# Second self attention: ScalarE seeds the score banks, and the values follow each slot

## The reference

```python
q = (h @ wq).reshape(b, n, 16, 64).transpose(0, 2, 1, 3)   # k and v alike, from the same h
scores = jnp.einsum('bhnd,bhld->bhnl', q, k) * 64 ** -0.5
probs = jax.nn.softmax(scores, axis=-1)
out = jnp.einsum('bhnl,bhld->bhnd', probs, v)
return out.transpose(0, 2, 1, 3).reshape(b, n, 1024) @ wo + bo
```

## Time and profile before

| What | Value |
|---|---|
| median of 3 runs | 4223.74 us |
| lowest and highest | 4218.38 and 4226.12 us |
| span of the profiled execution, first to last instruction | 4217.9 us |
| second self attention, first transfer to last projection (about) | 1905 to 3436 us |
| mean granted TensorE clock over the span | 0.952 |
| PE, DVE, ACT, POOL busy over the span | 93%, 66%, 44%, 44% |

### The profile page before, as it was taken

How to read it: one execution, slowest core, us unless ns; L and a number is a source line. 1 busy time by engine, 2 the same in 40 slices (tenths; PEclk the granted TensorE clock), 3 DMA queues, 4 the chain that set the end, 5 groups by cost and what they waited for, 6 DMA issues and landing times. The chain is left out here.

```text
span 4217.9 us, 64445 instructions
## 1 busy us (share of the span) xinstructions
PE 3909.5 (93%) x24639; PEld 2598.3 (62%) x24639; DVE 2770.9 (66%) x4547; ACT 1839.2 (44%) x2746; POOL 1859.2 (44%) x1203
## 2 busy tenths in 40 slices
PE   3799999994998997998999999999999979999899
PEld 2533443433557886884666666666666647777787
DVE  6599999953536654435676767676766737665665
ACT  1267777771443333442333333333333334444333
POOL 1288970001203002005777777877787753222200
PEclk9789999996779998997999999999999989999899
DMA  4734434405622005883211111121112010000100
GB/s 159 180 56 77 59 57 48 42 2 94 102 43 52 22 13 197 306 308 103 75 51 51 64 63 51 51 76 51 51 51 76 26 31 10 10 10 1 42 15 17
DMA packets 314421, 294.96 MB, mean 70 GB/s; under 512 B 133420, under 2 KB 237292, under 8 KB 313860
## 3 DMA queue, kind: packets, MB, share of 16 engines
q1 hardware_dynamic: 311460, 281.88, 25.7%
q0 software_dynamic: 2656, 8.97, 0.7%
HBM read 161.92 MB, written 127.28 MB: 69 GB/s over the span
## 5 line engine op out<-in xcount | busy, mean ns | idle before, releaser
L1741 POOL TENSOR_TENSOR f_sums<-f_sums,f_probs 128x1024 f32<-128x1024 f32 x384 | 915.5, 2384 | 154.8 <-ACT f_probs L1860 117.1
L1860 ACT ACTIVATE f_probs<-f_st 128x1024 f32<-128x1024 f32 x512 | 525.0, 1027 | 938.7 <-PE f_st L1906 933.9
L1758 DVE TENSOR_REDUCE f_mx<-f_s 128x1 f32<-128x512 f32 x1024 | 659.8, 686 | 380.7 <-PE f_s L1883 369.4
L1369 DVE TENSOR_REDUCE f_mx<-f_s 128x1 f32<-128x512 f32 x1024 | 638.6, 683 | 50.8 <-PE f_s L1501 28.4
L1481 ACT ACTIVATE f_probs<-f_st 128x512 f32<-128x512 f32 x1024 | 535.9, 601 | 225.6 <-PE f_st L1518 225.5
L1883 PE MATMUL f_s<-f_k,f_q 64*128 64x512 f32 x3072 | 515.0, 415 | 18.6 <-DMA f_k<-k 12.5
L1906 PE MATMUL f_st<-f_q,f_k 64*128 64x512 f32 x3072 | 485.2, 390 | 1.1 <-ACT f_probs L1860 1.0
L1920 PE MATMUL f_acc<-f_probs,f_v 128*64 128x512 f32 x2048 | 465.0, 596 | 0.0
L1883 PEld LDWEIGHTS f_s<-f_k,f_q 64*128 64x128 f32 x3072 | 341.2, 189 | 166.6 <-issue 112.1
L1906 PEld LDWEIGHTS f_st<-f_q,f_k 64*128 64x128 f32 x3072 | 366.4, 184 | 25.9 <-ACT f_probs L1860 3.8
L1518 PE MATMUL f_st<-f_q,f_k 50*128 50x512 f32 x1024 | 332.7, 472 | 6.9 <-ACT f_probs L1481 6.8
(11 more groups left out here) (320 smaller groups left out, 7874.5 us busy)
## 6 DMA issues: line engine op xcount, KB each, us to landing
q<-f_stage SPq DMA_DIRECT2D x80, 512.0 KB, 2.9
k<-f_stage SPq DMA_DIRECT2D x80, 512.0 KB, 2.9
f_q<-q SPq DMA_DIRECT2D x32, 1024.0 KB, 5.0
f_k<-k SPq DMA_DIRECT2D x32, 1024.0 KB, 7.3
v<-f_v_stage SPq DMA_DIRECT2D x64, 256.0 KB, 3.1
f_v<-v SPq DMA_DIRECT2D x32, 512.0 KB, 8.5
f_q<-q SPq DMA_DIRECT2D x96, 128.0 KB, 4.2
f_k<-k SPq DMA_DIRECT2D x96, 128.0 KB, 6.9
```

The source lines that it names most:

```text
L1369: v.tensor_reduce(mx[:, i % 2, c:c + 1], bank[u % 4][:, :], AX_X, ALU.max).then_inc(s_free, 1)
L1741: g_.tensor_tensor(out, out, probs[:, n % NP, :, :], ALU.add).then_inc(sum_done, 1)
L1758: v.tensor_reduce(mx[:, i % 2, c:c + 1], bank[u % 3][:, :], AX_X, ALU.max).then_inc(s_free, 1)
L1860: a_.activation(probs[:, s % NP, :, :], stb[s % 2][:, :, :], ACT.Exp, scale=L.scale).then_inc(p_ready, 1)
```

## The change

- `shifted` has 3 x 2 matmuls; the fourth product is gone, with `mones` and `m`. In its place ScalarE copies the negative maxima, held on all 128 partitions in `shift`, into the double bank (128 x 1024) after the exp that emptied it (`seed`), and the matmuls add to what stands there. `prime` issues four matmuls once at the start.
- `turned` is one copy on VectorE in place of two operations. `maxima` writes 8 KB to DRAM, waits, and then reads it back onto 128 partitions, 1 MB, by one transfer a step, in place of four small ones.
- GROUP goes from 4 to 1. TensorE's list for each slot is one shifted set, one pair, and the values of the slot two back. `weigh` stands in slots 1 and 9 behind the pair, the projections in slots 7 and 15 behind the pair, `turn` at the start of slot 8. The first values of a half stand in slots 2 and 10.
- EARLY goes from 3 to 8: pairs run up to 24 ahead, and 8 of step 1 are issued before the first slot.
- On VectorE the reciprocal stands behind the pair of its slot. q and k are loaded once the shifted sets of step i - 1 are issued, v once its values are done.

```diff
-        NP, DEPTH, GROUP, EARLY, RING0 = 8, 3, 4, 3, 3
+        NP, DEPTH, GROUP, EARLY, RING0 = 8, 3, 1, 8, 3
+        BLOCKS, PER_HALF, LAG = SLOTS // GROUP, KC // GROUP, 2
...
+        def next_pair(i, s):
+            n, j = (i + 1, EARLY + s) if s < SLOTS - EARLY else (i + 2, s - SLOTS + EARLY)
+            return (n, j) if n < STEPS else None
...
+        def turn_at(i, b):
+            return i + 1 if b == (SLOTS - EARLY) // GROUP and i + 1 < STEPS else None
...
+        def den_at(i, b):
+            if b == PER_HALF + 1:
+                return i, 0
+            return (i - 1, 1) if b == 1 and i > 0 else None
...
+        def y_at(i, b):
+            if b == BLOCKS - 1:
+                return i, 0
+            return (i - 1, 1) if b == PER_HALF - 1 and i > 0 else None
...
+        def values_at(i, b):
+            if b >= LAG:
+                return i, b - LAG
+            return (i - 1, BLOCKS + b - LAG) if i > 0 else None
...
-            m = [sb(f"m{k}", [P, N], F32R) for k in two]
-            mones = sb("mones", [P, P], F32R)
+            shift = [sb(f"shift{k}", [P, 2, N]) for k in two]
...
                 def maxima(i):
                     par = i % 2
-                    sp.wait_ge(m_split, i + 1)
-                    for h in range(2):
-                        for r in range(2):
-                            row = 64 * h + r
-                            sp.dma_start(m[par][row:row + 1, :].bitcast(F32).rearrange("o (q t) -> o q t", t=P),
-                                         mm[par][h * QB:(h + 1) * QB, r, :]).then_inc(m_in[par], 16)
+                    sp.wait_ge(s_free, at["turn", i] + 1)
+                    if i >= 2:
+                        sp.wait_ge(m_in[par], 16 * (i // 2))
+                    sp.dma_start(self.shift[par].rearrange("(c t) -> c t", t=P), mm[par][:, :]).then_inc(m_out[par], 16)
+                    sp.wait_ge(m_out[par], 16 * (i // 2 + 1))
+                    if i >= 2:
+                        sp.wait_ge(seeded, (i - 1) * SLOTS)
+                    sp.dma_start(shift[par][:, :, :].rearrange("p h t -> p (h t)"), self.shift[par].partition_broadcast(P))\
+                        .then_inc(m_in[par], 16)
...
-                sp.wait_ge(set_done, 6)
...
-                            sp.wait_ge(pv_done, i * GROUP)
+                            sp.wait_ge(st_ready, i * SLOTS)
                         load(i + 2)
+                        if i > 0:
+                            sp.wait_ge(pv_done, i * BLOCKS)
+                        load_values(i + 2)
...
-                        dve.wait_ge(m_in[par], i // 2 * 64)
-                    v.tensor_scalar(mm[par][:, 0, :].bitcast(U32), rows.bitcast(U32), HI12, None,
-                                    ALU.bitwise_and).then_inc(m_cut, 1)
-                    dve.wait_ge(m_cut, i + 1)
-                    v.tensor_tensor(mm[par][:, 1, :], rows, mm[par][:, 0, :], ALU.subtract).then_inc(m_split, 1)
-                    dve.wait_ge(m_split, i + 1)
-                    dve.sem_inc(s_free, 1)
+                        dve.wait_ge(m_out[par], 16 * (i // 2))
+                    v.tensor_copy(mm[par][:, :], rows).then_inc(s_free, 1)
...
-                    dve.wait_ge(pv_done, 2 * n + 2)
+                    dve.wait_ge(pv_done, (n + 1) * PER_HALF)
...
+                    for b in range(BLOCKS):
+                        if turn_at(i, b):
                             negate(i + 1)
+                            turned(i + 1)
+                        for s in range(GROUP * b, GROUP * b + GROUP):
+                            if next_pair(i, s):
+                                pair(*next_pair(i, s))
+                        if y_at(i, b):
+                            k, half = y_at(i, b)
+                            project(2 * k + half)
+                        if den_at(i, b):
+                            k, half = den_at(i, b)
+                            invert(2 * k + half)
+                        if values_at(i, b) and values_at(i, b)[1] % PER_HALF == PER_HALF - 1:
+                            k, grp = values_at(i, b)
+                            normalise(2 * k + grp // PER_HALF)
...
-                act.sem_inc(p_ready, 2)
...
+                def seed(n):
+                    i, s = n // SLOTS, n % SLOTS
+                    half = s // KC
+                    if n >= 2:
+                        act.wait_ge(p_ready, n - 1)
+                    if s == 0:
+                        act.wait_ge(m_in[i % 2], 16 * (i // 2 + 1))
+                    a_.activation(stb[s % 2][:, :, :], shift[i % 2][:, :, half * HALF:(half + 1) * HALF], ACT.Copy).then_inc(seeded, 1)
...
+                act.wait_ge(primed, 1)
+                seed(0)
+                seed(1)
...
                         a_.activation(probs[:, s % NP, :, :], stb[s % 2][:, :, :], ACT.Exp, scale=L.scale).then_inc(p_ready, 1)
-                        if s == 5 and i > 0:
+                        if n + 2 < STEPS * SLOTS:
+                            seed(n + 2)
+                        if s == 4 and i > 0:
                             high(2 * i - 1)
-                        if s == 13:
+                        if s == 12:
                             high(2 * i)
...
+                def prime():
+                    pe.wait_ge(q_in[0], 32)
+                    for k in two:
+                        for h in range(2):
+                            ins = t.matmul(stb[k][:, h, :], k_[0][:, 0, 0:P], q[0][:, 0, 0:HALF], start=True, stop=True)
+                    ins.then_inc(primed, 1)
...
                 def shifted(i, s):
-                    cur, par, half, c = i % DEPTH, i % 2, s // KC, s % KC
-                    if s == 0:
-                        pe.wait_ge(m_in[par], (i // 2 + 1) * 64)
-                    pe.wait_ge(p_ready, i * SLOTS + s + 1)
+                    cur, half, c = i % DEPTH, s // KC, s % KC
+                    pe.wait_ge(seeded, i * SLOTS + s + 1)
                     cols, keys = slice(half * HALF, (half + 1) * HALF), slice(c * P, (c + 1) * P)
-                    for r, (kk, qq) in enumerate(((0, 0), (0, 1), (1, 0), (None, None))):
+                    for r, (kk, qq) in enumerate(((0, 0), (0, 1), (1, 0))):
                         for h in range(2):
                             rows = slice(64 * h, 64 * h + 64)
-                            lhs = mones[rows, :] if kk is None else k_[cur][rows, kk, keys]
-                            rhs = m[par][rows, cols] if kk is None else q[cur][rows, qq, cols]
-                            ins = t.matmul(stb[s % 2][:, h, :], lhs, rhs, start=r == 0, stop=r == 3, tile_position=(64 * h, 0))
+                            ins = t.matmul(stb[s % 2][:, h, :], k_[cur][rows, kk, keys], q[cur][rows, qq, cols], start=False, stop=r == 2,
+                                           tile_position=(64 * h, 0), skip_group_check=True)
                     ins.then_inc(st_ready, 1)
...
-                    pe.wait_ge(p_ready, i * SLOTS + GROUP * grp + GROUP + 2)
-                    if grp % 2 == 0 and 2 * i + grp // 2 > 0:
-                        pe.wait_ge(on_done, 2 * i + grp // 2)
+                    pe.wait_ge(p_ready, i * SLOTS + GROUP * grp + GROUP)
+                    half = 2 * i + grp // PER_HALF
+                    if grp % PER_HALF == 0 and half > 0:
+                        pe.wait_ge(on_done, half)
...
+                prime()
...
                 for i in range(STEPS):
-                    for s in range(SLOTS):
-                        shifted(i, s)
-                        if s == 3 and i > 0:
-                            weigh(i - 1, 1)
-                            values(i - 1, 3)
-                        if s == 7:
-                            if i > 0:
-                                project(2 * i - 2)
-                            values(i, 0)
-                        if s == 11:
-                            weigh(i, 0)
-                            values(i, 1)
-                        if s == 15:
-                            if i + 1 < STEPS:
-                                turn(i + 1)
-                            if i > 0:
-                                project(2 * i - 1)
-                            values(i, 2)
-                        if s < SLOTS - EARLY:
-                            if i + 1 < STEPS:
-                                pair(i + 1, EARLY + s)
-                        elif i + 2 < STEPS:
-                            pair(i + 2, s - SLOTS + EARLY)
+                    for b in range(BLOCKS):
+                        if turn_at(i, b):
+                            turn(i + 1)
+                        shifted(i, b)
+                        if next_pair(i, b):
+                            pair(*next_pair(i, b))
+                        if y_at(i, b):
+                            k, half = y_at(i, b)
+                            project(2 * k + half)
+                        if den_at(i, b):
+                            weigh(*den_at(i, b))
+                        if values_at(i, b):
```

(17 more changed lines are left out.)

67 lines of the change are left out of this document (25 added, 42 removed).

## The result

The changed kernel takes 4456.98 us, the median of 4 runs (4446.76 to 4463.29); the kernel before took 4224.57 beside it. The ratio is 1.0553, with an interval of 1.0532 to 1.0573. The profiled execution took 4461.46 us with a span of 4459.2, so 241.3 us are to be found against the span before.

A forecast was written before the change was run, and what follows sets the result against it. TensorE's list, busy 1409.97 of 1410 us at full clock, was taken to set the end. Terms of -118 + 173 + 119 + 14 + 7 - 4 = +191 took the span from 4217.9 to 4409; forecast 4415 us, range 4290 to 4480.

The forecast's parts named there:

- Step 1: Shifted sets on TensorE: 512 slots lose one product for both heads, 118 us less.
- Step 2: Values behind each slot: 384 more round trips between 64-row and 64-column tiles at 0.45 us, 173 us more.
- Step 3: Handover of `acc` between halves: TensorE waits 1.89 us for VectorE's multiply, 63 times, 119 us more.
- The rival of the clock: A tenth of TensorE's work runs at 1.2 GHz because of gaps: 154 us more, 4569 us; chance 0.04.
- Step 4: The turn in slot 8: one more tile change and a wait for `negate`, 31 x 0.45 = 14 us more.
- Step 5: Start and end: five early pairs cost 7 us more, a shorter final wait for POOL saves 4 us.
- What was taken as free: ScalarE's seeds, taken as 1.03 us each, the shift through DRAM and POOL's adds were to add no time.
- no drain at this grain: Rival: all 512 round trips between tile shapes cost nothing, 4213 us; chance 0.08 with its weaker forms.
- the handover is hidden: Rival: the chain behind `weigh` is covered and step 3 is nothing, 4296 us; chance 0.08.
- ScalarE's pace: Rival: seeds of 2.5 us make ScalarE pace the slots, 4588 us; chance 0.03.
- a late shift: Rival: the shift lands 6 us late in each step, 4600 us; chance 0.03.

The follow-up runs named there:

- e6: The changed kernel's order with the fourth product and its rows m back in place of ScalarE's seeds: 4496.78 us, ratio 1.0655.
- e12: e11 plus two one-column matmuls of zero weights on 64-column tiles between shifted set and pair, in 14 of 16 slots: 4562.09 us, ratio 1.0808.
- e2: The changed kernel with eight products of zero weights per head ahead of the pair before each handover: 4376.34 us, ratio 1.0367.
- e11: e2 with one product of zero weights per head ahead of each handover instead of eight: 4374.69 us, ratio 1.0377.
- e3: The changed kernel with the first values of each half one slot later, beside the second ones: 4387.82 us, ratio 1.0403.
- e1: The changed kernel, but ScalarE copies `acc` to SBUF; the multiply reads that copy and the next values wait only for the copy: 4468.91 us, ratio 1.059.
- e5: e1 with the multiply of a half placed on VectorE behind the reduces of the following slot's pair: 4261.35 us, ratio 1.0104.
- e9: The changed kernel in two-slot blocks (pair, set, set, pair, values), multiply between the next block's first reduces, projections one block later: 4183.23 us, ratio 0.9918.
- after: The changed kernel itself, with no further edit, against the kernel before: 4456.98 us, ratio 1.0553.
- e7: The changed kernel with GROUP 4, bursts of four slots and then their values, seeds and EARLY 8 kept: 4627.31 us, ratio 1.0958.

## Why the prediction came out as it did

The direction and most of the size were right: forecast 4415, measured 4457. The 241 us of the span against the 191 of the sum, step by step:

- **Step 1, the product.** 512 x 0.231 = 118 us, as forecast: sets have six records, and e6, which puts the product back, has slots 0.24 longer.
- **Step 2, the changes of shape.** Right in kind, too dear in size. Slots start 2.60 us apart (sets at 2501.33, 2503.94 and 2506.54), and the pieces are worth 6 x 0.231 + 0.86 = 2.25. A trip so costs 0.36: 0.15 from values to set (1.01 for 0.86), 0.11 in the set (0.80 for 0.69) and 0.10 in the pair ahead of the values. The 0.20 on the way in, read ahead of `weigh`, was the term that was too large. With 0.36 for the new trips and 0.45 for the old, the step is 512 x 0.36 - 128 x 0.45 = 127 us for the 173 forecast. e12 measures 0.42 with a visit that also has a few ns of columns.
- **Step 3, the handover.** 128.2 us in 63 waits for 119 forecast, 2.01 each for 1.89. VectorE's chain took 5.38 for 5.48, and 0.15 more to the start of the values, which the forecast left out; PE had nothing to do from 3.52 for 3.59.
- **What step 3 left out: the clock.** This is the term that failed. The forecast took the clock as 1.00 and left its fall to a rival with 0.04, "as the row of the start shows that it takes much more idling than forecast". That row had PE two thirds busy; nothing in it said that less idling would be free. Behind 47 of 53 waits of 2.01 us TensorE runs at half clock for 3.4 us, at 1.5 us a time, and e2 and e11 give back 91.5 and 89.4 us of the span (80.6 and 82.3 of the median) by filling the wait or 0.23 us of it. The Trainium skill ("TensorE: Matmul & The Clock Gate", Why this matters for your kernels) warns that idle gaps between bursts of matmuls bring the slow clock back. The trace agrees in kind, but here shorter gaps than the page's rule names are enough: one of 2.01 us at a time, in e3 two of 0.5 and 0.8. The rival of the clock had the mechanism right, and its 154 us came from a guess that a tenth of the work would be slow.
- **Step 4, the turn.** The transpose starts at 2510.91 and the next set at 2511.12, without a wait, as `negate` had ended (0.18 from 2510.67) by then. 31 x 0.21 = 7 us for 14.
- **Step 5, start and end.** The first shifted set starts at 1951.32, before at 1951.85, with five more pairs ahead of it; but the stage's loads were issued 5.1 us earlier (1899.91 for 1904.98), so the pairs cost about 4.5 of the 7 forecast. At the end the wait for POOL's last sum is 0.6 us for 4.1, as forecast, but TensorE waits 10.6 us in 4 waits before projections, where before had one of 1.3.
- **What was taken as free.** It was: seeds of 1.03 us, the shift landed in 4.7 for the bound of 7.3, and no wait of TensorE for a seed among its waits of the stage.

Together -118 + 127 + 128 + 91 + 7 = 235 of 241. The other 6 are not the start: ahead of the first shifted set and behind the last one the kernel is 3 us shorter than before, and between them 245 longer. They were not separated further. Steps 2 and 4 were forecast 53 too high, step 3 nine too low, and the clock 91 too low. So the total was nearer than its parts by luck: an excess of 53 hid more than half of the clock.

Of the rivals, "no drain at this grain" is refuted by the slots of 2.60 us and by e12; "the handover is hidden" by the 63 waits; ScalarE's pace and a late shift by the seeds. The condition of the handover's rival, a VectorE free 1.9 us sooner, would not have been enough either: e1 and e3 took the wait from `acc`, and the three banks of `s` took it over, wholly or in part. Only with the multiply behind the reduces as well (e5) does the wait go.

## What to carry to other kernels

Cost a change of order by the changes of tile shape that it adds and by the reuse distance of every bank, not only of the one whose wait the profile shows: here saving a product worth 118 us brought about 346 us of changes, waits and slow clock. When a new idle gap recurs on TensorE, price the work behind it at half clock too, and try a cheap filler before a redesign. A fix that removes one wait must be checked for the next buffer in the same engine's queue; moving the multiply, the pairs and the projections, in blocks of two (e9), was what turned the same idea into 0.8% less time.

## What the runs showed of the hardware

- Granted clock, from 1970 to 3400. Slow stretches, nearly all of about 3.4 us, followed 47 of 53 waits of 2.01 us (after) and 45 of 52 of 1.90 us (e1), but only 3 of 52 of 1.76 us (e6), 1 of 50 of 1.78 us (e12) and none of 56 of 1.78 us (e11). In e3, where two waits of 0.5 and 0.8 us stand 0.5 us apart, there were 19. So no single length of a wait decides, and what does, these runs don't tell. In after the fall came 0.0 to 1.6 us after work had resumed; in e7, with waits of 4.0 us, mostly still in the wait, up to 2.0 us before its end.
- In e1 the multiply with both operands in SBUF took 2.20 us (median of 64; the fastest 0.69), where the one with an operand in PSUM, in after, took 0.69. POOL's timeline of e1 shows an add that reads SBUF in the same time:

```profile
2499.94 2.37 POOL L1769 TENSOR_TENSOR f_sums<-f_sums,f_probs 128x1024 f32<-128x1024 f32 x1 [1.01 <-ACT f_probs L1895]
```

The add ends at 2502.31 and the multiply, begun at 2500.66, at 2502.86, 0.55 later, as if it had run only then. In e1 and in e5, 63 of the 64 multiplies begin beside such an add, and all of these end 0.55 us behind it, whether they take 1.2, 2.2 or 2.4 us; the last one has no add beside it and takes 0.69. In after the same adds run beside 63 of the 64 multiplies, and every one takes 0.69. The Trainium skill ("SBUF — State Buffer", Who interferes with whom) has this rule: a VectorE instruction with two inputs in SBUF contends with a GpSimd one that reads SBUF. The trace agrees. So a copy out of PSUM can make the multiply behind it dearer.
- A change of shape from 64-row to 64-column tiles and back costs TensorE 0.36 us around the four value matmuls of a slot (after). Around four matmuls of one column it was 0.42 with these matmuls themselves (e12).
